# A decoder layer on one core: the last attention half by token tiles, and the sorted experts' fetches paced

## The chip, the cores and the metric

The kernel runs on one core of a Trainium2 chip. The metric is the device time of one execution in microseconds (us), the median of the runs shown; smaller is better.

## What is computed

The reference is one decoder layer for 2 x 512 tokens of width 512, all in float32:

```python
x = layernorm(x + ssm(x))                       # linear recurrence over the tokens
x = layernorm(x + cross_attention(x, context))  # 16 heads, 8 key heads, 1024 keys
h = x + self_attention(rmsnorm(x, norm1_w))     # causal, rope, 16 heads, 4 key heads
x = layernorm(h + moe(rmsnorm(h, norm2_w)))     # and here:

logits = xt @ gate_w                            # 8 experts
topv, topi = top_k(logits, 2); probs = softmax(topv)
for e in range(8):
    y = (silu(xt @ w1[e]) * (xt @ w3[e])) @ w2[e]   # width 1024
    out += w[:, e:e+1] * y                      # w: probs where e was chosen, else 0
```

## The kernel before

Matrix products are made of fp16 pairs: every operand is split into a high and a low fp16 part, and three products (high-high, high-low, low-high, `PAIRS`) are added in PSUM. So each operand costs a copy by ScalarE (high part), a subtraction by VectorE or GpSimd (low part), and, where it has to be turned, a DMA transpose issued by SyncE (SP). Every engine's program is written out by hand in Bass, with semaphores; nothing is scheduled by a tool. Phases (ssm, cross attention, self attention, routing, experts) end at a barrier.

**Self attention** (`attention`, called as "sa") works by halves: a half `h` is one key head `kv` and one sequence `b`, with four query heads (`groups`) of four token tiles of 128 (`TPB`), so `NS` = 16 steps `j`. A step makes the scores of one head and tile (`scores`, L1145, width 128 to 512 by the causal mask), the mask with the row's minimum (VectorE L1485), the exponential (ScalarE L1298), the reciprocal (L1446), its scale on GpSimd (L1007), the high part of the probabilities `PN` (ScalarE L1276) and the low one (VectorE L1453), and SP turns them into `PT` (L931). After every fourth step `values` (L1157) multiplies one head's turned probabilities with V, six steps (`TAIL`) behind; ScalarE (L1313) and VectorE (L1502) split the result into `OT`. A half also does jobs for its neighbours in fixed slots: the next half's projections, and the output of the half before (`output`, L1112), one tile of four heads a job, added to X by VectorE (`output_add`, L1435). In the last half (h = 7) there are no projections; the output of half 6 stands at `late_slots`, with three heads ahead (`parts_at`, steps 5 to 7) and the fourth later. WO of key head 3 is split in steps 0 to 3 of it (ScalarE L1281, GpSimd L981).

The half's own output can be finished only when all four heads are done, since `values` goes head by head: `first_parts` and `last_output` (L1121) gather it in four banks. Then for each tile: addition (L1435), mean square (ScalarE L1347, `row_square`), scale (GpSimd L1072 and L1074, `row_scale`), scaled row (VectorE L1524, `row_norm`), high part (ScalarE L1352, `row_high`), low part (VectorE L1530, `row_low`), turning by SP (L971), logits on TensorE (L1223) and the top two on VectorE (L1536 to L1543, `best_two`). Tiles 0 to 3 are sequence 0, whose rows are complete earlier; 4 to 7 are sequence 1. Before the turning, SP issues `next_loads`, the first expert's W1 and W3 (4 MB, L967, into `first`).

**Routing** ranks the choices. **The experts** (`phase_moe_routed`) are sorted by the number of their tokens, into places p = 0 to 7 with capacities of 352 down to 240 rows; the text calls them experts 1 to 8. GpSimd scatters the rows to DRAM (16 indirect DMAs, L1891) and then adds eight tiles (L1894). For each expert SP loads W13 of the next one (L1860), its rows (L1839), W2 (L1866), turns the rows (L1850) and stores the results (L1877). A step of an expert is `f`, one eighth of the width 1024: TensorE (L1936), Silu (ScalarE L2009), W2's high part (L2011), the product (VectorE L2067), W2's low part (L2070), and both parts of the result (L2019, L2078). The down projection (L1954, L1950) follows, tile by tile. In the last expert the results aren't stored but brought back by a matrix of `chosen` rows (VectorE L2084, turned by SP at L1872, L1972), while the other experts' rows are gathered from DRAM (16 indirect DMAs, L1907) and added by `combine` (L2055, L2058: tile t needs `gathered[t]`). `finish_rows` (L2117 to L2122) adds the last part and takes the statistics of the layer norm.

## Time and profile before

| | us |
|---|---|
| median of 3 runs | 1466.82 (1466.47 to 1468.64) |
| the profiled execution | 1465.96 |
| its span | 1464.3 |
| PE busy in it | 1324.5 (90%) |
| DVE, ACT, POOL busy | 1027.5, 808.1, 373.4 |
| mean granted clock of TensorE | 0.96 of full |

PE is the matmul engine TensorE, DVE is VectorE, ACT ScalarE, POOL GpSimd, SPq SP's queue of DMA issues. A row of a timeline gives the start in us from the beginning of the span, the time of the instruction or of several merged ones (x12), line and tiles (out<-in, buffer numbers left out), and in brackets how long the engine had been idle and what ended that. Matmuls overlap in the rows: twelve in a row are shown some 0.16 us longer than the distance to the next start. A label of a release is inferred from semaphores and can name the wrong DMA.

### The profile page before, as it was taken

The page shows a single profiled execution, that of the slowest core. Times are in us where ns is not written, and L with a number is a line of the kernel's source. Part 1 is how long each engine was busy: PE and PEld are TensorE (multiplying, and loading weights), DVE is VectorE, ACT ScalarE, POOL GpSimd, SP SyncE. Part 2 cuts the span into 40 slices and gives each one's busy share as a digit, 9 for nine tenths or more (in the row PEclk, how much of TensorE's full clock was granted, in tenths as well). Part 3 has the DMA queues.
Part 4 walks back from the last instruction along what each step waited for, and adds up shares of the span by engine and source line. Part 5 has one row for each costly group of instructions (what it writes and reads, how often), then busy time and mean ns, then how long its engine had stood idle before and what let it go on. Part 6 is the DMA issues. An engine that isn't in the chain of part 4 may idle for free. (4 is left out here: it accounts for less than half of the span.)

```text
span 1464.3 us, 24568 instructions
## 1 busy us (share of the span) xinstructions
PE 1324.5 (90%) x7943; PEld 715.8 (49%) x7943; DVE 1027.5 (70%) x1958; ACT 808.1 (55%) x1460; POOL 373.4 (25%) x610
## 2 busy tenths in 40 slices
PE   7988999999999999998688999998857999999965
PEld 4443444444444444443344555454434556666652
DVE  5847777777777777777568787878667556566646
ACT  5547666666666666665356565757523444555422
POOL 5402020202020202013456473645227000000042
PEclk9999999999999999999789999999878999999978
DMA  8327767676666666694643535335476646566751
GB/s 246 58 63 132 151 112 143 116 147 115 142 122 137 122 132 127 129 180 95 235 85 70 136 64 131 72 74 106 92 213 242 204 144 207 200 222 226 228 153 59
DMA packets 451836, 206.18 MB, mean 141 GB/s; under 512 B 401056, under 2 KB 415392, under 8 KB 451744
## 3 DMA queue, kind: packets, MB, share of 16 engines
q1 hardware_dynamic: 448608, 196.67, 56.9%
q0 software_dynamic: 2560, 8.39, 1.9%
q8 instruction: 44, 0.72, 0.2%
q14 instruction: 48, 0.39, 0.1%
q10 hardware_dynamic: 576, 0.00, 0.0%
HBM read 87.38 MB, written 16.45 MB: 71 GB/s over the span
## 5 line engine op out<-in xcount | busy, mean ns | idle before, releaser
L1453 DVE SCALAR_TENSOR_TENSOR X<-xa_SC,xa_rs,X 128x1024 f16<-128x1024 f32 x128 | 164.3, 1283 | 98.3 <-issue 97.6
L1276 ACT ACTIVATE X<-xa_SC,xa_rs 128x1024 f16<-128x1024 f32 x128 | 147.1, 1149 | 110.5 <-POOL xa_rs L1007 110.5
L1145 PE MATMUL xa_psS<-xa_KT,xa_QT 128*128 128x512 f16 x768 | 186.4, 379 | 6.0 <-DVE xa_mn L1485 4.6
L1157 PE MATMUL xa_psO<-wide,xa_V 128*128 128x512 f16 x768 | 173.8, 383 | 7.2 <-DMA wide<-X 6.9
L1007 POOL TENSOR_SCALAR xa_rs<-xa_rc,flag 128x1 f32<-128x1 f32 x128 | 33.9, 265 | 517.0 <-DVE xa_rc L1446 517.0
L1485 DVE CUSTOM_DVE_ANT_0 xa_SC<-xa_psS,maskb 128x1024 f32<-128x1024 f32 x128 | 155.0, 1211 | 4.5 <-PE xa_psS L1145 2.4
L1298 ACT ACTIVATE xa_SC<-xa_SC,xa_mn 128x1024 f32<-128x1024 f32 x128 | 145.4, 1136 | 13.4 <-DVE xa_mn L1485 13.3
L1936 PE MATMUL rmoe_psG<-rmoe_XGT,W 128*128 128x352 f16 (+6 forms) x768 | 112.9, 298 | 17.1 <-DVE zeros L2067 8.1
L1157 PEld LDWEIGHTS xa_psO<-wide,xa_V 128*128 128x128 f16 x768 | 74.5, 98 | 102.6 <-issue 17.5
L1936 PE MATMUL rmoe_psU<-rmoe_XGT,W 128*128 128x352 f16 (+6 forms) x768 | 112.7, 296 | 7.1 <-issue 7.0
L1145 PEld LDWEIGHTS xa_psS<-xa_KT,xa_QT 128*128 128x128 f16 x768 | 73.3, 98 | 90.7 <-DVE xa_mn L1485 9.4
L1298 ACT ACTIVATE sa_SC<-sa_SC,sa_mn 128x128 f32<-128x128 f32 (+3 forms) x128 | 71.4, 558 | 79.2 <-DVE sa_mn L1485 79.1
L1954 PE MATMUL rmoe_psY<-W,rmoe_HT 128*128 128x512 f16 (+3 forms) x456 | 99.9, 379 | 0.8 <-DVE rmoe_HT L2078 0.8
L1088 PE MATMUL xa_psJ<-XT,xa_WP 128*128 128x512 f16 x384 | 89.9, 385 | 11.0 <-POOL xa_WP L981 8.4
L1936 PEld LDWEIGHTS rmoe_psG<-rmoe_XGT,W 128*128 128x128 f16 x768 | 76.0, 100 | 46.0 <-DVE zeros L2067 9.4
L1088 PE MATMUL sa_psJ<-XT,first 128*128 128x512 f16 x384 | 92.4, 394 | 5.8 <-PEq L57 3.9
L1112 PE MATMUL sa_psJ<-sa_WO,sa_OT 128*128 128x512 f16 x336 | 79.5, 386 | 15.2 <-POOL sa_WO L981 7.0
L1453 DVE SCALAR_TENSOR_TENSOR sa_PN<-sa_SC,sa_rs,sa_PN 128x128 f16<-128x128 f32 (+3 forms) x128 | 77.5, 606 | 21.8 <-issue 9.9
L1936 PEld LDWEIGHTS rmoe_psU<-rmoe_XGT,W 128*128 128x128 f16 x768 | 76.3, 99 | 32.9 <-issue 8.8
L1112 PE MATMUL xa_psJ<-xa_WO,xa_OT 128*128 128x512 f16 x360 | 87.6, 379 | 0.0
L1485 DVE CUSTOM_DVE_ANT_0 sa_SC<-sa_psS,causal 128x128 f32<-128x128 f32 (+3 forms) x128 | 61.8, 483 | 36.1 <-PE sa_psS L1145 32.4
L1276 ACT ACTIVATE sa_PN<-sa_SC,sa_rs 128x128 f16<-128x128 f32 (+3 forms) x128 | 71.0, 555 | 27.2 <-POOL sa_rs L1007 24.8
(291 smaller groups left out, 2273.9 us busy)
## 6 DMA issues: line engine op xcount, KB each, us to landing
first<-in_L_ffn_w_dram SPq DMA_DIRECT2D x14, 2048.0 KB, 11.9
W2raw<-in_L_ffn_w_dram SPq DMA_DIRECT2D x8, 2048.0 KB, 9.1
expert_rows_dram<-zeros SPq DMA_DIRECT2D x10, 512.0 KB, 9.7
xa_WPraw<-in_L_xattn_Wq_dram SPq DMA_DIRECT2D x8, 512.0 KB, 11.1
xa_WOraw<-in_L_xattn_Wo_dram SPq DMA_DIRECT2D x8, 512.0 KB, 4.7
first<-in_L_ffn_wq_dram SPq DMA_DIRECT2D x4, 1024.0 KB, 8.0
first<-in_L_ffn_wo_dram SPq DMA_DIRECT2D x4, 1024.0 KB, 5.7
first<-in_L_ffn_w_dram SPq DMA_DIRECT2D x8, 512.0 KB, 6.8
```

What stands on the lines that cost most here:

```text
L1007: nc.gpsimd.tensor_scalar(rs[:, j % 4:j % 4 + 1], rc[:, j % 4:j % 4 + 1], unit, 1.0, ALU.mult, ALU.mult).then_inc(scale_done, 1)
L1088: last = nc.tensor.matmul(bank[:, :], wq_v[:, hw, k, a, :], XT[:, hx, k, b * S:(b + 1) * S], start=(q + k == 0), stop=(q == 2 and k == DC ...
L1112: last = nc.tensor.matmul(bank[:, :], OT[b][:, ho, g, t * P:(t + 1) * P], WO[:, hw, g, :], start=(g + q == 0), stop=(g == groups - 1 and q ...
L1145: last = nc.tensor.matmul(psS[j % NSC][:, c:c + cw], QT[b][:, hq, g, t * P:(t + 1) * P], KT[b][:, hk, c:c + cw], start=(q == 0), stop=(q = ...
L1157: last = nc.tensor.matmul(psO[:, c:], V[b][:, hv, blk, :], PT[g % NPT][:, blk, hp, c:], start=(blk + q == 0), stop=(blk == NBLK - 1 and q ...
L1276: nc.scalar.activation(PN[j % NPN][:, 0:w // P, 0, :], by_block(SC[j % NSC], w), ACT.Identity, scale=rs[:, j % 4:j % 4 + 1]).then_inc(norm ...
L1298: nc.scalar.activation(SC[j % NSC][:, 0:w], SC[j % NSC][:, 0:w], ACT.Exp, bias=mn[:, j % 4:j % 4 + 1], scale=-1.0, accum_out=sm[:, j % 4:j ...
L1453: nc.vector.scalar_tensor_tensor(out=PN[j % NPN][:, 0:w // P, 1, :], in0=by_block(SC[j % NSC], w), scalar=rs[:, j % 4:j % 4 + 1], in1=PN[j ...
L1485: nc.vector.tensor_tensor_reduce(out=SC[j % NSC][:, 0:w], in0=psS[j % NSC][:, 0:w], in1=mask_of(b, j % TPB), scale=-SCORE_SCALE, scalar=3e ...
L1936: last = nc.tensor.matmul(bank[f % 2][:, 0:c], W13[:, hw, w, k, f * P:(f + 1) * P], XGT[:, hx, k, 0:c], start=(i + k == 0), stop=(i == 2 a ...
L1954: last = nc.tensor.matmul(psY[y][0:w, :], HT[:, hh, k, r * P:r * P + w], W2[:, hw, k, :], start=(i + k == 0), stop=(i == 2 and k == FC - 1))
```

## The change

It has two parts. In the self attention's last half the steps go by token tile: `step_of` gives tile 3 with its four heads first, then tiles 2, 1 and 0. `tile_values` multiplies one tile of all four heads, `own_output` makes its output one tile later, and square, scale, norm, parts and logits of the tiles follow in tables of steps (`square_at` and so on); the order of the tiles in them is `tile_of`. The turned probabilities of tiles 3 and 1 lie in `first`, so `next_loads` wait for the third tile's values. The output of half 6 is made whole, in slots 8 to 11.

In the experts, the second expert's W13 is fetched in four pieces, each after the one before; the rows of the next expert are turned ahead of W2's fetch; `chosen` is made and turned in experts 2 to 5 in place of the last; a tile's gathers wait for those two tiles before; and `combine` is spread over the last expert and behind it. ScalarE waits for W2 after the first Silu.

```diff
@@ attention
-    late_slots = {8: ([("wo", 0)], []), 9: ([("wo", 1)], []), 10: ([("wo", 2)], []), 12: ([("wo", 3)], [])}
-    parts_at = {5: 0, 6: 1, 7: 2}
+    late_slots = {8 + t: ([("wo", t)], []) for t in range(TPB)}
...
+        PT_last = PT if route is None else [
+            ap.bitcast(F16).rearrange("p (k l c) -> p k l c", l=2, c=S)
+            for ap in (route[-1][:, 0:NBLK * S], turned[:, 0].rearrange("p t d -> p (t d)"))]
...
-            square_at = (11, 12, 13, 14)
+            tile_of = [0, 1, 2, 3, 7, 6, 5, 4]
...
+            own_bank = [psJ[i] for i in (1, 0, 2, 1)]
+            square_at = {10: 0, 11: 1, 12: 2, 13: 3, 16: 4, 18: 5, 20: 6}
+            high_at = {14: 0, 15: 1, 16: 2, 17: 3, 18: 4, 19: 5}
+            scale_at = {11: 0, 12: 1, 13: 2, 14: 3}
+            own_at = {15: 0, 17: 1, 20: 2}
+            norm_at = {13: 0, 14: 1, 15: 2, 16: 3, 17: 4, 18: 5}
+            low_at = {14: 0, 15: 1, 16: 2, 17: 3, 18: 4, 20: 5}
...
+        def step_of(m, last):
+
+            j = m % NS
+            return (j % groups, TPB - 1 - j // groups) if by_tile(m, last) else (j // TPB, j % TPB)
...
@@ SyncE, attention
                 sp.wait_ge(wo_done, kv_heads * NWO)
-                sp.wait_ge(job_ready, jobs_before(last_h))
+                sp.wait_ge(pv_ready, last_h * groups + 3)
                 for dst, src, arrived in next_loads:
                     sp.dma_start(dst, src).then_inc(arrived, 16)
-                for i in range(NT):
-                    sp.wait_ge(xp_lo, i + 1)
+                for n, i in enumerate(tile_of):
+                    sp.wait_ge(xp_lo, n + 1)
...
@@ TensorE, attention
+            def tile_values(h, b, u):
+
+                for q in range(TPB):
+                    pe.wait_ge(landed[q], 16 * (h * groups + u + 1))
+                wait_from(pe, o_lo, h * groups + u)
+                t = TPB - 1 - u
+                for blk in range(t + 1):
+                    for q, (hv, hp) in enumerate(PAIRS):
+                        last = nc.tensor.matmul(psO[:, :], V[b][:, hv, blk, :], PT_last[u % NPT][:, blk, hp, :],
+                                                start=(blk + q == 0), stop=(blk == t and q == 2))
+                last.then_inc(pv_ready, 1)
+
+            def own_output(h, b, u):
+                output(h, b, TPB - 1 - u, last_job(TPB + u), own_bank[u], NJ, h * groups + u)
...
-                    if causal and last and j in parts_at:
-                        k = parts_at[j]
-                        pe.wait_ge(wo_done, kv_heads * NWO)
-                        output(h - 1, 1 - b, k, jobs_before(h) + k, psJ[BANK[b][k]], jobs_back(h, k, last),
-                               range(groups - 1))
                     m = j - TAIL
                     if m % TPB == TPB - 1 and (m >= 0 or not first):
-                        values(head_of(h, m), b if m >= 0 else 1 - b, (m % NS) // TPB)
+                        if by_tile(m, last):
+                            if m // TPB == TPB - 1:
+                                logits(0)
+                            tile_values(h, b, m // TPB)
+                        else:
+                            values(head_of(h, m), b if m >= 0 else 1 - b, (m % NS) // TPB)
+                        if by_tile(m, last) and m > TPB:
+                            own_output(h, b, m // TPB - 1)
...
@@ SyncE, experts
                     for i, w in enumerate((w1, w3)):
-                        sp.dma_start(W13raw[:, i, :, :], w[bass.ds(named[p], 1)].rearrange("o (k p) f -> p (o k) f", p=P)).then_inc(w13_in, 16)
+                        rows = w[bass.ds(named[p], 1)].rearrange("o (k p) f -> p (o k) f", p=P)
+                        if first:
+                            for k in range(0, DC, 2):
+                                wait_from(sp, w13_in, 16 * (2 * i + k // 2))
+                                sp.dma_start(W13raw[:, i, k:k + 2, :], rows[:, k:k + 2, :]).then_inc(w13_in, 16)
+                        else:
+                            sp.dma_start(W13raw[:, i, :, :], rows).then_inc(w13_in, 16)
...
                     load_rows(p + 1)
+                    turn_rows(p + 1)
                     sp.wait_ge(w2_done, FC * (p + 1))
                     sp.dma_start(W2raw[:], w2[bass.ds(named[p], 1)].rearrange("o (k p) d -> p (o k) d", p=P)).then_inc(w2_in, 16)
-                    turn_rows(p + 1)
-                if last:
-                    for t in range(NT):
+                if p in choose_at:
+                    for t in choose_at[p]:
                         sp.wait_ge(chosen_done, t + 1)
...
@@ GpSimd, experts
             for t in range(NT):
+                if t >= 2:
+                    pool.wait_ge(gathered[t - 2], 32)
                 for k, dst in enumerate((Y1, Y2)):
                     pool.indirect_dma_start(out=dst[:, t, :], out_offset=None, in_=YG[0:ROWS, :],
...
@@ VectorE, experts
+                    if p in choose_at and f < len(choose_at[p]):
...
                     if last and f >= FC // 2:
-                        for t in range(2 * f - FC, 2 * f - FC + 2):
-                            combine(t)
+                        combine(f // 2 - 2, f % 2)
+                if last:
+                    combine(2)
+                    combine(3)
                 for r in range(TILES[p]):
                     if last:
...
-                        if r:
+                        if r == 0:
+                            for t in range(4, 7):
+                                combine(t)
+                        else:
                             finish_rows(r - 1)
...
             over_experts(dve, step)
+            combine(NT - 1)
             for t in range(TILES[LAST] - 1, NT):
                 finish_rows(t)
```

`choose_at` is two tiles in each of the places 1 to 4.

The order of TensorE's program at the end of the last half, before (`sa_psO` are values, `sa_WO` outputs, `sa_GWP` logits; four rows of values are one head):

```order
L1157 MATMUL sa_psO<-wide,sa_V 128x128 x3
L1121 MATMUL sa_psS<-sa_WO,sa_OT 128x512 x3
L1121 MATMUL sa_psJ<-sa_WO,sa_OT 128x512 x3
L1121 MATMUL sa_psS<-sa_WO,sa_OT 128x512 x3
L1121 MATMUL sa_psJ<-sa_WO,sa_OT 128x512 x15
L1223 MATMUL sa_psS<-sa_GWP,XT 128x8 x84
L1223 MATMUL sa_psO<-sa_GWP,XT 128x8 x12
```

and the same place now:

```order
L1206 MATMUL sa_psS<-sa_KT,sa_QT 128x128 x6
L1177 MATMUL sa_psO<-first,sa_V 128x512 x6
L1143 MATMUL sa_psJ<-sa_WO,sa_OT 128x512 x12
L1196 MATMUL sa_psS<-sa_GWP,XT 128x8 x48
L1177 MATMUL sa_psO<-wide,sa_V 128x512 x3
L1143 MATMUL sa_psJ<-sa_WO,sa_OT 128x512 x24
L1196 MATMUL sa_psS<-sa_GWP,XT 128x8 x36
L1196 MATMUL sa_psO<-sa_GWP,XT 128x8 x12
```

All logits stood behind all values and outputs; now those of the first four tiles (x48) stand ahead of the last tile's values (x3) and of the last two outputs (x24).

SP's program in the loop's place 2 (it fetches for the next expert, of 304 rows), before:

```order
L1860 DMA first<-in_L_ffn_w_dram 128x4x1024 x2
L1839 DMA X<-expert_rows_dram 128x2x512
L1842 DMA X<-expert_rows_dram 48x512
L1866 DMA W2raw<-in_L_ffn_w_dram 128x8x512
L1850 DMA_TRANSPOSE rmoe_XGT<-X 128x8x128 x3
L1877 DMA expert_out_dram<-X 128x512 x2
```

and now:

```order
L1925 DMA first<-in_L_ffn_w_dram 128x4x1024 x2
L1898 DMA X<-expert_rows_dram 128x2x512
L1901 DMA X<-expert_rows_dram 48x512
L1909 DMA_TRANSPOSE rmoe_XGT<-X 128x8x128 x3
L1932 DMA W2raw<-in_L_ffn_w_dram 128x8x512
L1937 DMA_TRANSPOSE wide<-wide 128x3x128 x2
L1942 DMA expert_out_dram<-X 128x512 x2
```

The turning of the rows stands ahead of W2's fetch, and two transposes of `chosen` (`wide`) have come in behind it.

## Rows read from the trace of the kernel before

**Rows 1.** The page, its first line.

```profile
span 1464.3 us, 24568 instructions
```

**Rows 2.** Windows: us, busy us by engine, granted clock, DMA share, GB/s.

```profile
1068.00:1090.00 22.00, 4.97 (x133) 4.25 (x133) 12.25 (x55) 3.77 (x10) 4.63 (x29) 0.61 0.86 192
...
1392.00:1429.00 37.00, 25.59 (x193) 20.27 (x194) 16.57 (x35) 8.25 (x20) 15.70 (x16) 0.77 0.56 143
```

**Rows 3.** Timeline of PE in the last half: start, us, what, idle before.

```profile
1026.16 4.02 PE L1112 MATMUL sa_psJ<-sa_WO,sa_OT 128*128 128x512 f16 x9 [7.02 <-POOL sa_WO L981]
...
1042.86 2.75 PE L1112 MATMUL sa_psJ<-sa_WO,sa_OT 128*128 128x512 f16 x12
```

**Rows 4.** Timeline of SP's queue behind the last half.

```profile
1057.48 4.11 SPq L967 DMA_DIRECT2D first<-in_L_ffn_w_dram  x8
1061.70 17.87 SPq L971 DMA_TRANSPOSE XT<-wide  x8
```

**Rows 5.** Timeline of DVE: norm and low parts of the first four tiles.

```profile
1056.57 1.40 DVE L1524 SCALAR_TENSOR_TENSOR wide<-X,sa_rr,sa_wb 128x512 f32<-128x512 f32 x2
...
1059.08 2.49 DVE L1530 TENSOR_TENSOR wide<-wide 128x512 f16<-128x512 f32 x4
```

**Rows 6.** Timeline of PE: logits of the first and the fourth tile.

```profile
1071.78 0.44 PE L1223 MATMUL sa_psS<-sa_GWP,XT 128*128 128x8 f16 x12 [4.22 <-DMA XT<-wide]
...
1076.87 0.48 PE L1223 MATMUL sa_psS<-sa_GWP,XT 128*128 128x8 f16 x12 [2.45 <-DMA XT<-wide]
```

**Rows 7.** Timeline of DVE: last addition, last low part, top two.

```profile
1069.46 0.68 DVE L1435 TENSOR_TENSOR X<-sa_psJ,X 128x512 f32<-128x512 f32 x1
...
1074.31 0.69 DVE L1530 TENSOR_TENSOR wide<-wide 128x512 f16<-128x512 f32 x1 [0.68 <-ACT wide L1352]
...
1082.68 0.16 DVE L1543 FIND_INDEX8 idx<-top,lg 128x8 uint32<-128x8 f32 x1
```

**Rows 8.** Timelines of ACT, DVE, POOL and PE in the first expert.

```profile
1118.29 0.46 ACT L2009 ACTIVATE ropeC<-rmoe_psG 128x352 f32<-128x352 f32 x1 [5.23 <-DMA wide<-sa_PN]
...
1119.29 10.63 DVE L2070 TENSOR_TENSOR W<-W2raw,W 128x512 f16<-128x512 f32 x1
...
1119.56 9.80 POOL L1894 TENSOR_TENSOR X<-X 128x512 f32<-128x512 f32 x8
...
1130.85 3.55 PE L1936 MATMUL rmoe_psG<-rmoe_XGT,W 128*128 128x352 f16 x12 [7.51 <-DVE zeros L2067]
```

**Rows 9.** Timelines of PE and SP's queue at the start of expert 8.

```profile
1392.02 1.41 PE L1936 MATMUL rmoe_psG<-rmoe_XGT,W 128*128 128x240 f16 x12 [2.37 <-DMA rmoe_XGT<-X]
...
1381.49 8.48 SPq L1850 DMA_TRANSPOSE rmoe_XGT<-X  x2
```

**Rows 10.** Timelines of ACT, PE, SP's queue and POOL in expert 8.

```profile
1403.63 0.37 ACT L2009 ACTIVATE ropeC<-rmoe_psG 128x240 f32<-128x240 f32 x1 [5.25 <-DMA wide<-sa_PN]
...
1418.05 0.37 ACT L2009 ACTIVATE ropeS<-rmoe_psG 128x240 f32<-128x240 f32 x1 [13.19 <-DMA wide<-sa_PN]
...
1410.19 0.76 PE L1936 MATMUL rmoe_psU<-rmoe_XGT,W 128*128 128x240 f16 x3 [1.95 <-issue]
...
1434.41 5.99 PE L1954 MATMUL rmoe_psY<-W,rmoe_HT 128*128 128x512 f16 x27 [0.83 <-DVE rmoe_HT L2078]
...
1397.11 25.76 SPq L1872 DMA_TRANSPOSE wide<-wide  x8
...
1414.17 0.95 POOL L1907 DMA_INDIRECT XT<-expert_out_dram,rmoe_slots  x1 [0.30 <-issue]
```

**Rows 11.** Groups by line and form, 1389 to 1441: busy us, mean ns.

```profile
L2055 DVE SCALAR_TENSOR_TENSOR X<-wide,p,X 128x512 f32<-128x512 f32 x8 | 6.0, 745 | 0.0
```

**Rows 12.** Windows, columns as rows 2: during the sixteen scatters.

```profile
1104.00:1108.00 4.00, 4.00 (x19) 2.20 (x18) 3.82 (x7) 1.42 (x3) 3.69 (x2) 0.65 0.34 131
```

**Rows 13.** DMA issues: what, count, KB each, median us to landing.

```profile
expert_out_dram<-X SPq DMA_DIRECT2D x14, 256.0 KB, 2.5
...
XT<-wide SPq DMA_TRANSPOSE x8, 3.3
```

More of the change, by code:

```diff
@@ L1104, in project, with output @@
                 last.then_inc(job_ready, 1)
-            def output(h, b, t, job, bank, back=NJ, gs=range(groups)):
-                pe.wait_ge(o_lo, h * groups + gs[-1] + 1)
+            def output(h, b, t, job, bank, back=NJ, head=None):
+                pe.wait_ge(o_lo, (h + 1) * groups if head is None else head + 1)
                 wait_from(pe, job_free, job - back + 1)
-                for g in gs:
+                for g in range(groups):
                     for q, (ho, hw) in enumerate(PAIRS):
@@ L1137, in first_parts, with logits @@
                     last_output(t, early)
+            def tile_values(h, b, u):
[10 more added lines that the diff above has]
+                output(h, b, TPB - 1 - u, last_job(TPB + u), own_bank[u], NJ, h * groups + u)
+            def logits(n):
+                lo, hi, bank = choice[n]
+                if n == 0:
+                    pe.wait_ge(gw_done, 1)
+                    pe.wait_ge(masked, (last_h + 1) * NS)
+                first_tile = min(tile_of[lo:hi])
+                for i in tile_of[lo:hi]:
+                    pe.wait_ge(xt_in[i], 16)
+                    for q, (hx, hw) in enumerate(PAIRS):
+                        for k in range(DC):
+                            at = (i - first_tile) * E
+                            last = nc.tensor.matmul(bank[:, at:at + E], XT[:, hx, k, i * P:(i + 1) * P], GWP[:, hw, k, :],
+                                                    start=(q + k == 0), stop=(q == 2 and k == DC - 1))
+                last.then_inc(logits_ready, 1)
             def scores(n, b, g, t, j):
@@ L1168, in jobs @@
                         pe.wait_ge(wo_done, (kv + b) * NWO)
-                        output(h - 1, 1 - b, i, job, psJ[BANK[b][k]], jobs_back(h, k, last),
-                               range(groups - 1, groups) if causal and last and i in parts_at.values() else range(groups))
+                        output(h - 1, 1 - b, i, job, psJ[BANK[b][k]], jobs_back(h, k, last))
             def half(h, kv, b, first, last):
@@ L1479, in half @@
                     if j < NS:
-                        w = width(j % TPB)
+                        t = step_of(j, last)[1]
+                        w = width(t)
                         dve.wait_ge(scores_ready, n + 1)
@@ new lines, in half, with own_add, row_norm @@
+                    if last and route is not None and j in own_at:
+                        own_add(own_at[j])
+                    if last and route is not None and j in norm_at:
+                        row_norm(norm_at[j])
+            def own_add(u):
+                output_add(last_h, 1, TPB - 1 - u, last_job(TPB + u), own_bank[u])
+            def row_norm(n):
+                if n == 0:
+                    dve.wait_ge(wb_in, 16)
+                if n == 7:
+                    dve.wait_ge(xp_lo, 5)
+                dve.wait_ge(rr_done, n + 1)
+                dve.wait_ge(job_free, last_job(n) + 1)
+                nc.vector.scalar_tensor_tensor(out=xw[n], in0=X[:, tile_of[n], :], scalar=rr[:, n:n + 1], in1=wb[:],
@@ L1541, in best_two @@
                 dve.wait_ge(top_done, n + 1)
-                for i in range(lo, hi):
+                for i in tiles:
                     last = nc.vector.max_index(idx[:, i, :], top[:, i, :], lg[:, i, :])
@@ L2385, in decoder_layer @@
                   turned=wide[:, :, TPB:, :],
-                  route=(norm2_w, XW, XP, gate_w, lg, top, idx, next_loads, zeroed, 16 * len(cleared), kept))
+                  route=(norm2_w, XW, XP, gate_w, lg, top, idx, next_loads, zeroed, 16 * len(cleared), kept, first))
         W13 = sb("W13", [P, 2, 2, DC, F], F16)
```

250 lines of the change are left out of this document (120 added, 130 removed).

## The prediction

> **What bounds the kernel now.** I read the page first: one core, span 1464.3 us [rows 1]. The profiled execution took 1465.96 us, 1.7 over its span and 0.9 under the median of 1466.82; the sum is made against 1465.96, and 0.9 is added at the end. A measurement of this kernel tells a change from none from about 0.2%, 2.9 us.
>
> The chain of waits runs through TensorE for most of the experts, and the table by stage says where it does not: in 1068 to 1090 PE works 4.97 of 22 us, and in 1392 to 1429, the last expert, 25.59 of 37 [rows 2]. I therefore read the timelines around these two and at the two ends of the change. The reader is to see five things. (a) In the last half of the self attention PE stands 7.02 us for the split of WO (POOL L981), and its next nine matmuls take 4.02 us; twelve take 2.75 elsewhere, 2.59 or 0.216 each from start to start [rows 3]. (b) SP issues the 4 MB of the first expert's weights from 1057.48 and the turned rows of the norm behind them; though four tiles were ready at 1061.6 (DVE L1530 ends), they reach PE only at 1071.78 (first) and 1076.87 (fourth) [rows 4, 5, 6]. (c) From the last output's addition to the end of the top two there are 13 us in which almost nothing but latency passes [rows 7]. (d) In the first expert ScalarE gets its third step 5.23 us late, and one DVE instruction of some 0.69 us takes 10.63, as long as POOL's eight additions beside it [rows 8]. (e) Expert 8 starts 2.37 us late for its rows [rows 9], then ScalarE stands 5.25 and 13.19 us on something the trace can't name (the transposes in the label were long over), with PE doing single matmuls between "issue" gaps; SP's eight transposes of `chosen` and POOL's sixteen gathers are in flight then [rows 10].
>
> **The sum, part by part.** A, B, C, D are the terms.
>
> *A, attention by tiles.* Softmax, values and outputs hold the same columns as before; only their order moves. The stall of 7.02 us goes, since no output stands at step 5 any more. What is late next: the four widest tiles now come first, each with a piece of WO, at some 1.9 us a step (ScalarE 0.72 + 0.61 + 0.51), then four at 1.3; DVE has the last head of the half before at about 1029.3. Only then can PE's first output begin. From there PE is full: four outputs at 2.59, values 2.59 and 1.94, the first own output 2.59, scores 1.5, and 1.7 for the half clock after the idle time (row 1026.16: 9 matmuls 4.02 for 1.94, less what a shorter idle time saves): 20.7, so 1050.0. DVE then has four masks, reciprocals and low parts of width 128 (2 us), the low part of OT 0.6, four low parts and three norms of rows at 0.62 and 0.70 [rows 5], one addition: 6.8, so 1056.8. SP turns the last tile (1.2) and begins the loads at 1058.1, where it was 1057.48: the time won at (a) is used up, **+0.6**.
>
> The price is behind that. `next_loads` now wait for the third tile's values because that tile lies in their destination, and `logits(0)` stands ahead of `tile_values` of the last tile in PE's program. It needs the turned rows of four tiles, which stand behind 4 MB in SP's order. Before, the fourth was there 1076.87 - 1057.48 = 19.4 us after the first load [rows 4, 6]; nothing about the loads has changed, so I take 19.4. Before, PE had no attention work left behind this wait. Now all of the following stands there: logits 0.5; values and own output 2, 15 matmuls at 0.216 plus 2.0 for the half clock, 5.3 (25.2 so far); addition 0.7, square 0.8 (ScalarE has it ahead of OT's high part), OT high 0.6, low 0.65 (27.9); own output 3, 2.6; addition 0.7 (31.2); square to low part 4.9, the interval from 1070.14 to 1075.00 [rows 7]; turning 3.5, as XT's 3.3 [rows 13] and a semaphore; logits 0.5 and top two 0.7: 41.0 after the first load. Before: 1082.84 - 1057.48 = 25.4. **A = 0.6 + 15.6 = +16.2 us.** Bounds: if XT's rows weren't held, PE would take PV at 1061 and the chain end at 79.9, A = -2.9; if the first load begins 6 us later than reckoned (steps at 2.2), +22.
>
> *B, first expert.* The 4 MB for expert 2 come in four pieces, one at a time. If ScalarE's third step is no longer late, DVE has multiplied step 3 (0.53) before POOL's additions begin at 1119.56, and PE does step 5 in their shadow; the next begins where step 5 began, 1130.85 [rows 8]. That is one step of two groups of 1.8 (expert 8's 1.23 by 352/240 columns), **-3.6**. Bounds 0 and -7.5 (PE's whole idle time). The additions themselves stay. For these the Trainium skill (SBUF — State Buffer, "SBUF: two separate sides") says that DVE and GpSimd take the shared port for one whole instruction and the other blocks; by that a DVE instruction would wait one addition of 1.2 us, and B would be near -7.5. The row shows it blocked through all eight, and the measurement decides.
>
> *C, rows turned ahead of W2.* Expert 8's 2.37 us go: its transposes took 8.48 us in issue behind 2 MB of W2 [rows 9]. **-2.4**; W2 itself is issued some 3 us later (2 or 3 transposes at 1.3) and has the down projection, 10.4 us or more, to land in before ScalarE's first piece, which now comes after the first Silu: nothing. The two transposes of `chosen` in experts 2 to 5 stand before the stores of YR and the next W13 load, but the turning ahead of them no longer stands behind W2 either: I put SP 1 us later there, ahead of loads that have a whole up projection to land, at nothing (at most 1 us at each of four experts). DVE's `chosen`, 0.42 each, lies in PE's steps of 3.1 to 3.6.
>
> *D, last expert.* From 1392.02 PE needs eight steps of 2.46 (two groups of twelve matmuls, 1.41 less an overlap of 0.18 [rows 9]) and 48 matmuls of 0.216, 19.7 + 10.4 = 30.1; it ended at 1440.24 (1434.41 + 5.99 less the overlap [rows 10]), 48.2 later: 18.1 too much. Two causes: the waits of (e), and DVE's four `combine` in each of the steps 4 to 7 (3.0 us beside 1.3 of other work, against 2.46 of PE). Both go: one combine (0.75) beside the 1.3 fits into 2.46; tiles 2 to 6 fall under the down projection; tile 7's two, 1.4, come on DVE's last chain [rows 11]. **-18.1 + 1.4 = -16.7.** The transposes are gone from here, and scatters of the same form alone kept the DMA engines 0.34 busy, while PE ran full [rows 12]; so I take the waits as gone. Bounds: +1.4 (all stay) and -16.7. The pacing allows two tiles in flight. A gather's landing isn't shown; stores of the same 256 KB took 2.5, turned rows 3.3 [rows 13]. Up to 3.3 the window of two tiles costs nothing (POOL issues one tile in 2.5); at 5 it gives a tile each 3.75, tile 6 at 1425 in place of 1418, and costs 6.
>
> Sum: 16.2 - 3.6 - 2.4 - 16.7 = **-6.5**: 1459.5, with 0.9 a median of **1460**.
>
> **Rivals.** (1) *The rows aren't held:* XT lands soon after its issue, as PN does. Against it [rows 4, 6]. It gives -2.9 - 22.7 = -25.6, 1441.
> (2) *Slower: instructions still come late in the last expert.* If the gathers from POOL alone, and not they with the transposes, keep ScalarE and PE waiting, the 18.1 us stay: +16.2 - 6.0 + 1.4 = +11.6, 1479. It decides once more than 9.4 of the 18.1 stay. For it: ScalarE's long wait (1404.9 to 1418.05) ends 3 us after the last gather was issued. Against it: [rows 12].
> (3) *The window is too narrow:* gathers take 5 us, +6, 1466.
> (4) *Pacing does nothing for another queue:* each DMA engine takes turns between queues, so ScalarE's wait in expert 1 would not depend on how many pieces of W13 stand behind each other; B is 0: 1464. The Trainium skill states such turns (DMA: Bandwidth & Descriptors, "Queues, rings and completion order": "each SDMA engine round-robins between the queue rows it has work for, at *packet* granularity"). No row of the trace before tells the two apart.
>
> **How the numbers follow.** My forecast 0.45, its own range 1451 to 1469 (A by 5 either way, B by 4); rival 1 0.15, rival 2 0.15, rival 3 0.10, rival 4 0.10; 0.05 for a first load far later. Faster by over 2.9: four fifths of mine, rival 1, half of 4, a little of 3: 0.58. Slower by over 2.9: rival 2, a tenth of mine, some of 3 and the 0.05: 0.24. Within: 0.18. The range leaves out half of rival 1 and most of 2: 1441 to 1474.
>
> **What would show it.** First W13 load at 1055 to 1061; PE idle some 17 us before `logits(0)`, with the last tile's values behind it; top two end near 1099. After that everything counted from there: expert 2's up projection 3.6 us sooner, no PE idle time ahead of expert 8, no "issue" rows in it, PE 30 us from its first up to its last down matmul, and finish_rows(7) some 45 us after its start. If the rows of four tiles are there before the third tile's values end, A is wrong; if ScalarE stands in expert 8, D is.

## The result and the profile after

The changed kernel took 1480.54 us (median of 4 runs, 1478.91 to 1482.74) against 1466.64 for the kernel before, measured beside it: a ratio of 1.0103 (95% interval 1.0079 to 1.0127). It is slower by 1%, where I forecast 1460 and put 0.24 on slower. The profiled execution took 1478.91.

The page after, its first line; before it was 1464.3 [rows 1], so 12.7 us are to be found:

```profile
span 1477.0 us, 24551 instructions
```

The two traces have the same landmarks, and the 12.7 us are the differences of the stretches between them:

| stretch | before | after | change | forecast |
|---|---|---|---|---|
| A: to the end of the top two | 1082.84 | 1104.63 | +21.8 | +16.2 |
| B: from there to expert 1's end | 75.88 | 72.24 | -3.6 | -3.6 |
| C: from there to expert 8's first matmul | 233.30 | 230.40 | -2.9 | -2.4 |
| D: expert 8, first up to last down matmul | 48.22 | 43.75 | -4.5 | -18.1 |
| D: from there to the end | 24.06 | 25.98 | +1.9 | +1.4 |

A single stretch has some play: in the other traces of this record the top two end at 1099.6 to 1103.8 with the changed attention (e1, e14, e16) and at 1082.7 to 1086.7 with that of before (e2, e5 to e8, e10 to e12). So A is some 13 to 22 us, and 21.8 between these two traces; e1's time (19.4 us over before, with 3.2 won back in B) speaks for the upper end.

**A.** PE's timeline after, at the end of the attention (start, us, what, idle before):

```profile
1033.29 2.75 PE L1143 MATMUL sa_psJ<-sa_WO,sa_OT 128*128 128x512 f16 x12 [2.06 <-issue]
...
1055.29 2.75 PE L1143 MATMUL sa_psJ<-sa_WO,sa_OT 128*128 128x512 f16 x12
1079.46 0.46 PE L1196 MATMUL sa_psS<-sa_GWP,XT 128*128 128x8 f16 x12 [21.42 <-DMA XT<-wide]
...
1082.98 0.48 PE L1196 MATMUL sa_psS<-sa_GWP,XT 128*128 128x8 f16 x12 [0.85 <-DMA XT<-wide]
1083.33 1.44 PE L1177 MATMUL sa_psO<-wide,sa_V 128*128 128x512 f16 x3
1084.56 4.23 PE L1143 MATMUL sa_psJ<-sa_WO,sa_OT 128*128 128x512 f16 x12
1091.54 4.14 PE L1143 MATMUL sa_psJ<-sa_WO,sa_OT 128*128 128x512 f16 x12 [2.75 <-DVE sa_OT L1553]
...
1103.47 0.49 PE L1196 MATMUL sa_psO<-sa_GWP,XT 128*128 128x8 f16 x12 [5.92 <-DMA XT<-wide]
```

and SP's queue beside it:

```profile
1053.36 10.97 SPq L957 DMA_TRANSPOSE wide<-sa_PN  x4
1064.43 4.03 SPq L993 DMA_DIRECT2D first<-in_L_ffn_w_dram  x8
1068.58 33.02 SPq L997 DMA_TRANSPOSE XT<-wide  x8
```

PE stands 21.4 us ahead of `logits(0)`, with the last tile's values, two outputs and half of the rows' chain behind it in its program. The fourth tile's rows came 18.55 us after the first load (19.4 before, [rows 4, 6]).

**B.** DVE's timeline after, in the first expert:

```profile
1141.43 10.26 DVE L2137 TENSOR_TENSOR W<-W2raw,W 128x512 f16<-128x512 f32 x1
```

and PE's:

```profile
1152.62 3.51 PE L2003 MATMUL rmoe_psG<-rmoe_XGT,W 128*128 128x352 f16 x12 [5.07 <-DVE causal L2134]
```

DVE is blocked through POOL's eight additions as in [rows 8]; PE's idle time is 5.07 in place of 7.51, and it has one step more behind it when it comes.

**D.** PE's timeline after, in expert 8:

```profile
1407.27 1.39 PE L2003 MATMUL rmoe_psG<-rmoe_XGT,W 128*128 128x240 f16 x12
...
1421.24 0.47 PE L2003 MATMUL rmoe_psU<-rmoe_XGT,W 128*128 128x240 f16 x3 [0.18 <-issue]
1422.64 0.47 PE L2003 MATMUL rmoe_psU<-rmoe_XGT,W 128*128 128x240 f16 x3 [0.93 <-issue]
...
1424.07 0.57 PE L2003 MATMUL rmoe_psU<-rmoe_XGT,W 128*128 128x240 f16 x4 [0.44 <-issue]
1429.91 2.28 PE L2003 MATMUL rmoe_psG<-rmoe_XGT,W 128*128 128x240 f16 x10 [5.27 <-DVE causal L2134]
1433.22 0.36 PE L2003 MATMUL rmoe_psG<-rmoe_XGT,W 128*128 128x240 f16 x1 [1.03 <-issue]
...
1440.66 10.52 PE L2021 MATMUL rmoe_psY<-W,rmoe_HT 128*128 128x512 f16 x48
1451.02 1.03 PE L2039 MATMUL rmoe_psG<-X,wide 128*128 128x512 f16 x4
```

ACT's, the Silu of the steps 5 and 6:

```profile
1429.04 0.37 ACT L2071 ACTIVATE ropeC<-rmoe_psG 128x240 f32<-128x240 f32 x1 [9.38 <-DMA wide<-sa_PN]
...
1435.52 0.37 ACT L2071 ACTIVATE ropeS<-rmoe_psG 128x240 f32<-128x240 f32 x1 [5.24 <-DMA wide<-sa_PN]
```

POOL's, the first and the last of the sixteen gathers:

```profile
1412.75 1.00 POOL L1974 DMA_INDIRECT wide<-expert_out_dram,rmoe_slots  x1 [259.44 <-DMA expert_out_dram<-X]
...
1432.09 0.95 POOL L1974 DMA_INDIRECT XT<-expert_out_dram,rmoe_slots  x1 [0.30 <-issue]
```

Expert 8 starts without idle time, and the transposes of `chosen` are gone from it. Yet the same picture as in [rows 10] is back: single matmuls between "issue" gaps and ScalarE late without a cause that the trace names (at 1429.04 PE's product had been complete since 1424.6), from 8 us after the first gather's issue to 3 us after the last one's.

### The profile page after: what moved, and what is told of

The parts are those of the page before. It is cut to its first block and busy times, and to the rows that moved or that the text cites. A ratio compares the mean times of both kernels' runs of the same rounds, so it can differ in the third digit from the quotient of the medians.

```text
span 1477.0 us, 24551 instructions
## 1 busy us (share of the span) xinstructions
PE 1324.3 (90%) x7925; PEld 716.1 (48%) x7925; DVE 1027.6 (70%) x1958; ACT 808.2 (55%) x1460; POOL 371.7 (25%) x610
## 5 line engine op out<-in xcount | busy, mean ns | idle before, releaser
L1351 ACT ACTIVATE xa_SC<-xa_SC,xa_mn 128x1024 f32<-128x1024 f32 x128 | 145.4, 1136 | 14.4 <-DVE xa_mn L1535 14.3
L1143 PE MATMUL sa_psJ<-sa_WO,sa_OT 128*128 128x512 f16 x384 | 91.0, 388 | 13.3 <-DVE sa_OT L1553 8.7
L1502 DVE SCALAR_TENSOR_TENSOR sa_PN<-sa_SC,sa_rs,sa_PN 128x128 f16<-128x128 f32 (+3 forms) x128 | 77.1, 602 | 20.9 <-issue 10.6
L2003 PEld LDWEIGHTS rmoe_psU<-rmoe_XGT,W 128*128 128x128 f16 x768 | 75.5, 98 | 26.8 <-issue 3.6
L1329 ACT ACTIVATE sa_PN<-sa_SC,sa_rs 128x128 f16<-128x128 f32 (+3 forms) x128 | 71.1, 555 | 28.5 <-POOL sa_rs L1033 26.4
```

The source lines that it names most:

```text
L1143: last = nc.tensor.matmul(bank[:, :], OT[b][:, ho, g, t * P:(t + 1) * P], WO[:, hw, g, :], start=(g + q == 0), stop=(g == groups - 1 and q ...
L1329: nc.scalar.activation(PN[j % NPN][:, 0:w // P, 0, :], by_block(SC[j % NSC], w), ACT.Identity, scale=rs[:, j % 4:j % 4 + 1]).then_inc(norm ...
L1351: nc.scalar.activation(SC[j % NSC][:, 0:w], SC[j % NSC][:, 0:w], ACT.Exp, bias=mn[:, j % 4:j % 4 + 1], scale=-1.0, accum_out=sm[:, j % 4:j ...
L1502: nc.vector.scalar_tensor_tensor(out=PN[j % NPN][:, 0:w // P, 1, :], in0=by_block(SC[j % NSC], w), scalar=rs[:, j % 4:j % 4 + 1], in1=PN[j ...
L2003: last = nc.tensor.matmul(bank[f % 2][:, 0:c], W13[:, hw, w, k, f * P:(f + 1) * P], XGT[:, hx, k, 0:c], start=(i + k == 0), stop=(i == 2 a ...
```

## Experiments

Theories at the start: **held rows** (A is the time for which the 4 MB hold the rows, times PE's order), **gathers** (my rival 2: the gathers alone keep PE and ScalarE waiting), against **steps** (A is lost in the half itself) and **transposes and gathers together** (my forecast). The runs were made in five groups, each with its own runs of the kernel before; ratios are to these. Stage D means expert 8 from its first up to its last down matmul.

### The two parts apart

e1 keeps the changed attention and takes the experts from before; e2 the reverse. The edit is one half of the change's diff each: e1 leaves out all hunks on the experts, e2 all on the attention.

> The changed attention with the experts of before. Theory H (held rows): the whole loss is made in the attention; the top two end 21.7 us later than before (1082.84 to 1104.56 in the two traces) and nothing of it comes back, so 1466.6 + 21.7 = 1488. Rival: part of the 21.7 us overlaps with waits of the old experts (the first expert's idle 7.5 us), then 1480 to 1484.

> The attention of before with the changed experts. If the two parts add: the traces give 12.7 - 21.7 = -9.0, so 1466.6 - 9.0 = 1457.6, with 3.6 of it in the first expert, 2.9 ahead of expert 8 and 2.5 in and behind it. Rival: the gain in the first expert came only from the shifted place of the scatters in time; then 1461.

e1: 1485.3, ratio 1.0135 (1.01 to 1.0171); e2: 1459.8, 0.9954 (0.994 to 0.9968); the kernel before in this group 1465.89. The loss is the attention's and the experts' part does win. In e1 the top two end at 1103.78, 20.9 later than before, and stretch B is 72.7, that is 3.2 shorter than before **with the old experts**. PE's timeline in e1's first expert:

```profile
1142.77 1.96 PE L1994 MATMUL rmoe_psG<-rmoe_XGT,W 128*128 128x352 f16 x12 [0.72 <-DVE zeros L2125]
...
1151.53 3.70 PE L1994 MATMUL rmoe_psG<-rmoe_XGT,W 128*128 128x352 f16 x12 [5.01 <-DVE causal L2125]
```

and SP's, where both halves of the next W13 go out at once:

```profile
1133.62 0.54 SPq L1918 DMA_DIRECT2D first<-in_L_ffn_w_dram  x2
```

ScalarE waited long once here too (4.25 us), one step later, where it costs PE 0.72. In e2, with the pacing, it waited 5.18 us and PE 0.67. Nor is the pacing enough: e7 and e12 (below) have it, their third step comes late as before (waits of 5.73 and 5.72 us), and B is 75.7 and 75.5 as before. So B's 3.6 us aren't shown to come from the pacing: which of ScalarE's steps is late decides, and that differs from kernel to kernel. With the third late B is 75.5 to 75.9 (before, e7, e12), with the fourth 72.7 to 73.2 (e1, e2, e3). C's 3 us do come with the experts' part: 233.4 in e1, 230.4 in every kernel that has it. Stage D is 48.4 in e1 and 44.1 in e2.

### What held the attention

e3 issues the loads behind four tiles' turning; e4 moves the logits behind the outputs.

```diff
@@ e3: SyncE
-                for dst, src, arrived in next_loads:
-                    sp.dma_start(dst, src).then_inc(arrived, 16)
                 for n, i in enumerate(tile_of):
+                    if n == 4:
+                        for dst, src, arrived in next_loads:
+                            sp.dma_start(dst, src).then_inc(arrived, 16)
                     sp.wait_ge(xp_lo, n + 1)
@@ e4: TensorE
                         if by_tile(m, last):
-                            if m // TPB == TPB - 1:
-                                logits(0)
                             tile_values(h, b, m // TPB)
...
-                for n in range(1, len(choice)):
+                for n in range(len(choice)):
                     logits(n)
```

In e4 VectorE's `best_two(0)` and `best_two(1)` move behind `row_low(7)` as well.

> The changed kernel with the 4 MB of the first expert issued behind the turning of the first four tiles' rows. Theory H: the rows land some 1.3 us apart from 1065 on, logits(0) run at about 1070 in place of 1079 to 1083, and the last tile's values follow; the rows of the next tiles are then held to about 19 us behind the first load (1070 + 19 = 1089). Top two end near 1092, 12 us sooner: 1468. Rival S (the rows are late for another reason than the loads, for example the transposes' own queue): PE idles to 1079 as now, 1480.

> The changed kernel with logits(0) behind the last own output in TensorE's program, and the top two of all tiles at the end of VectorE's. Theory H: the loads still hold the rows, but values and outputs of the last tiles run beside them, so the end is 25.4 us behind the first load as before: 1064.4 + 25.4 = 1089.8, 14.7 us sooner than 1104.56: 1466. Rival S: the last rows stay late for their own chain (addition, square, scale, low part), and the top two end at about 1100: 1476.

e3: 1468.79, ratio 1.0014 (0.9997 to 1.0032); e4: 1463.46, 0.9986 (0.997 to 1.0001). The top two end at 1093.4 and 1090.5 in place of 1104.6. PE's timeline in e3, the logits of the first and the fourth tile:

```profile
1066.88 0.46 PE L1197 MATMUL sa_psS<-sa_GWP,XT 128*128 128x8 f16 x12 [9.87 <-DMA XT<-wide]
...
1070.94 0.48 PE L1197 MATMUL sa_psS<-sa_GWP,XT 128*128 128x8 f16 x12 [0.81 <-DMA XT<-wide]
```

and in e4, the last tile's values and the first logits:

```profile
1066.90 1.44 PE L1177 MATMUL sa_psO<-wide,sa_V 128*128 128x512 f16 x3 [8.13 <-DVE sa_OT L1551]
...
1079.79 0.44 PE L1196 MATMUL sa_psS<-sa_GWP,XT 128*128 128x8 f16 x12 [0.39 <-DMA XT<-wide]
```

With the loads behind them, the first rows reach PE 3.4 us after their transpose's issue (SP at 1063.47) in place of 10.9: it is the 4 MB that hold them. With the logits last the hold costs PE nothing, and the end is 25.4 us after the first load (1090.54 - 1065.13), the interval of the kernel before. Held rows and TensorE's order are shown for 14.1 of A's 21.8 us (1104.63 less 1090.54); the other 7.7 are the late first load, and these are lost in the half itself, as "steps" had it. e15 is e4 with the row work two steps later:

```diff
-            square_at = {10: 0, 11: 1, 12: 2, 13: 3, 16: 4, 18: 5, 20: 6}
-            high_at = {14: 0, 15: 1, 16: 2, 17: 3, 18: 4, 19: 5}
+            square_at = {10: 0, 11: 1, 12: 2, 13: 3, 16: 4, 18: 5, 21: 6}
+            high_at = {16: 0, 17: 1, 18: 2, 19: 3, 20: 4, 21: 5}
...
-            norm_at = {13: 0, 14: 1, 15: 2, 16: 3, 17: 4, 18: 5}
-            low_at = {14: 0, 15: 1, 16: 2, 17: 3, 18: 4, 20: 5}
+            norm_at = {15: 0, 16: 1, 17: 2, 18: 3, 19: 4, 20: 5}
+            low_at = {16: 0, 17: 1, 18: 2, 19: 3, 20: 4, 21: 5}
```

> The kernel of e4_logits_last with norm, high and low part of the rows of tiles 0 to 3 two steps later each (1 step for the square of the third own tile). Theory V (VectorE's and ScalarE's work on these rows, in between the masks and low parts of the last tile, makes the first load 7 us later than before): the last tile's turning ends some 3 us sooner, first load at about 1062 in place of 1065.1, and since the rows held behind it end 25.4 us after it, 1460. Rival: the first load is late for TensorE's outputs ahead of it; then it stays at 1065 and the time at 1463.

e15 ran in the fourth group: 1444.35, ratio 0.997 (0.9956 to 0.9983). SP's queue in e14 of the same group (with the rows' work where the change has it):

```profile
1050.53 10.96 SPq L957 DMA_TRANSPOSE wide<-sa_PN  x4
1061.59 4.00 SPq L993 DMA_DIRECT2D first<-in_L_ffn_w_dram  x8
```

and in e15:

```profile
1050.19 7.44 SPq L957 DMA_TRANSPOSE wide<-sa_PN  x4
1057.74 4.33 SPq L993 DMA_DIRECT2D first<-in_L_ffn_w_dram  x8
```

The turning of the last tile waited for its own low parts, which stood behind norms and low parts of rows on VectorE; without them it takes 3.5 us less. The first load comes 3.9 sooner, and 3.5 of that is the edit's: from the end of the first own output to the first load it is 12.3 us in the change, e4, e14 and e16, and 8.8 in e15 and e18. The top two end 25.5 us behind it again.

### What keeps the last expert waiting

All of these start from e2. e5 leaves the gathers out, e6 and e7 change the window, e8 and e12 fetch the same bytes plainly, e10 and e11 keep fewer gathers in flight. e5, e8 and e12 leave out or replace the rows that the layer needs, so they tell where time goes and are no kernels to keep; each has two runs:

```diff
@@ e6 (e7: neither line)
-                if t >= 2:
-                    pool.wait_ge(gathered[t - 2], 32)
+                if t >= 1:
+                    pool.wait_ge(gathered[t - 1], 32)
@@ e11
+                lag = 1 if t < 5 else 2
+                if t >= lag:
+                    pool.wait_ge(gathered[t - lag], 32)
@@ e10, with a semaphore for each k and t
                 for k, dst in enumerate((Y1, Y2)):
+                    if t >= 1:
+                        pool.wait_ge(gathered[k][t - 1], 16)
@@ e12 in place of the indirect DMA; e8 the same by SyncE
+                    at = (2 * t + k) * P
+                    pool.dma_start(dst[:, t, :], YG[at:at + P, :]).then_inc(gathered[t], 16)
```

> The kernel of e2_experts_only without its sixteen gathers (what is left out: the rows of the other experts aren't fetched, the additions take what lies in their buffers). Theory G: the gathers alone keep TensorE and ScalarE waiting in the last expert; from its first up matmul to the end of the down projection 30 us in place of 44.1, no issue rows, 1459.8 - 14 = 1446. Rival: the instructions come late for another reason (the place in the program); the stage stays at 44 and the time at 1459.

> The kernel of e2_experts_only with the gathers of one tile in flight in place of two. Theory Q (what waits behind the gathers waits the longer the more of them are outstanding): the stage shrinks from 44.1 to about 38, 1454. Rival T (only the bytes moved count): the stage stays within 1 us of 44.1; and if a tile's round trip gets longer than its 2.5 us of issue, the gathers end later and the time goes up to 1463.

> The kernel of e2_experts_only with all gathers issued without a wait, as before the change. Theory Q: the stage grows from 44.1 to 47 or more (it was 48.2 before, with the transposes beside the gathers), 1463. Rival T: 44.1 and 1460; then the 4.1 us came from the transposes and the spread additions alone.

> The kernel of e2_experts_only with sixteen plain fetches of 256 KB from SyncE's queue in place of the gathers, two tiles in flight (the rows fetched are not the chosen ones). If the bytes on the DMA engines are what keeps the others waiting (T): the stage stays near 44. If it is the kind of transfer that GpSimd issues row by row: the stage is near 30 and the time near 1446, as without gathers.

> The kernel of e2_experts_only with each gather waiting for the one two before it, so that two gathers are in flight all the time (in e6_one_tile two were issued and both had to land). Theory W (how many gathers stand in the queue decides): TensorE runs as in e6_one_tile, 30 us from its first up to its last down matmul, and the gathers need 16 x 2.0 = 32 us in place of 42, so the end comes 8 us sooner than in e6: 1450. Rival: a steady stream of gathers does what four in flight do, issue rows come back and the time stays at 1457 to 1460.

> The kernel of e2_experts_only with one tile in flight for the first five tiles and two for the last three, which fall into and behind the down projection. Theory W: TensorE is not held in the up projection, the last gather lands some 7 us sooner than in e6_one_tile: 1451. Rival: the last three tiles hold the down projection's instructions and the time stays at 1457.

> The fetches of e8_plain_fetches issued by GpSimd in place of SyncE (the rows fetched are not the chosen ones). If a transfer whose packets GpSimd's own queue moves is what delays the others: issue rows in the last expert and about 1459. If only the indirect form does: 30 us for the stage and 1446, as in e8.

| kernel | gathers in flight | stage D | from D to the end | median | ratio (interval) |
|---|---|---|---|---|---|
| e5 | none | 30.04 | 25.6 | 1444.77 | 0.9841 (0.9817 to 0.9865) |
| e6 | 2, both to land | 30.04 | 40.7 | 1457.63 | 0.9926 (0.9908 to 0.9943) |
| e7 | no limit set | 44.87 | 26.4 | 1462.04 | 0.9962 (0.9949 to 0.9976) |
| e8 | plain, SyncE | 30.04 | 26.1 | 1445.59 | 0.9847 (0.9823 to 0.9871) |
| e10 | 2, rolling | 30.04 | 30.1 | 1447.56 | 0.9869 (0.9837 to 0.99) |
| e11 | 2, from tile 5 on 4 | 30.04 | 33.5 | 1451.99 | 0.9893 (0.9876 to 0.9909) |
| e12 | plain, GpSimd | 30.04 | 26.2 | 1446.38 | 0.9852 (0.9832 to 0.9872) |

Without gathers the stage takes the 30.04 us that TensorE needs. So the 14 us of e2 are theirs alone, as rival 2 had it. (Before the change the stage took 48.2 us, and 48.4 in e1; the 3.5 more than e7's 44.87, which also sets no limit, belong to the transposes of `chosen` or to the four additions a step, which no run tells apart.) It is not their bytes: e8 moves the same 4.2 MB at the same place, and e12 even through the same queue and with the same number of packets. The DMA view of e12, 1392 to 1425 (packets, MB, share of 16 engines; KB each, us to landing):

```profile
q0 software_dynamic: 1280, 4.20, 40.6%
...
wide<-expert_out_dram POOLq DMA_DIRECT2D x8, 256.0 KB, 3.3
```

and of e2, 1394 to 1418:

```profile
q0 software_dynamic: 1280, 4.20, 61.4%
...
wide<-expert_out_dram,rmoe_slots POOLq DMA_INDIRECT x8
```

The indirect form, issued as fast as in e2 and e7, delays PE and ScalarE; with two in flight it doesn't. I had expected a slope (38 us in e6, 47 or more in e7), and that was wrong. e2's window and no window differ by only 0.8 us (44.06, 44.87), but they are nearly the same experiment: the sixteen issues of e2 span 19.6 us and those of e7 19.1, so a window of four hardly held anything back. In e6 and e10 the number in flight and the pace fall together (one gather in 2.6 and 1.9 us in place of 1.3), and no run tells which of the two matters. For plain fetches the pace doesn't: e8 and e12 issue theirs in 14.4 and 16.4 us. What is won is partly paid at the end (column four; e6's profiled execution took 1462.76, 5 over its median), since fewer in flight take longer, and the last tiles' additions stand ahead of `finish_rows`. PE's timeline behind stage D in e6:

```profile
1435.05 1.03 PE L1981 MATMUL rmoe_psG<-X,wide 112*128 112x512 f16 x2 [13.64 <-DVE X L2103]
```

and in e10:

```profile
1421.89 1.04 PE L1981 MATMUL rmoe_psG<-X,wide 112*128 112x512 f16 x2 [4.67 <-DVE X L2103]
```

In e6 a tile takes 5.1 to 5.5 us (1400.92, 1406.04, 1411.25, 1416.75), in e10 a gather lands 3.7 us after its issue and one goes out every 1.9.

### Half the loads, and both

e9 is e2 with W1 (4 of the 8 loads) ahead of the turning of the rows and W3 behind it; e13 and e17 are e9 with e10's gathers.

```diff
-                for dst, src, arrived in next_loads:
+                for dst, src, arrived in next_loads[:DC]:
                     sp.dma_start(dst, src).then_inc(arrived, 16)
                 for i in range(NT):
...
+                for dst, src, arrived in next_loads[DC:]:
+                    sp.dma_start(dst, src).then_inc(arrived, 16)
```

> The kernel of e2_experts_only (attention of before) with W1 of the first expert (2 MB) issued where all 4 MB were, and W3 behind the last turning of rows. Theory H: half the bytes hold the rows half as long; the first four tiles' rows land near 1069, the last ones some 4 us behind their low part, and the top two end 3 to 4 us sooner; W3 lands before the experts begin: 1459.8 - 3.5 = 1456. Rival: W3 lands too late for ScalarE's split and the gain is given back, 1459 to 1461.

e9: 1457.19, ratio 0.9928 (0.9911 to 0.9944); the top two end at 1081.45, 21.7 after the first load, where it was 25.4 before and 27.2 in e2. Stretch B is 71.8 as in e10 (71.9), so W3 isn't late. The intervals of e9 and e2 (another group) overlap at their ends, so the times alone don't show the gain; the traces do: from the first load to the top two it is 21.6 to 21.9 us in e9, e13 and e17, and 24.7 or more in all nine with the whole 4 MB ahead and the attention of before.

> e9_half_the_loads and e10_rolling_two together: the attention of before with half of the first expert's loads behind the rows, the changed experts with two gathers always in flight. The two edits lie 300 us apart, so they should add: 1447.6 - 2.6 = 1445. Rival: the last expert begins at another point of the instruction stream and some of the wait comes back, 1448 or more.

> The changed kernel with two gathers always in flight, nothing else. If what the gathers cost doesn't depend on the attention: as e2_experts_only to e10_rolling_two, 12.2 us less: 1480.5 - 12.2 = 1468, still level with before, the 21.7 us of the attention being left. Rival: less than 8 us, because the cost depends on where the expert's stage falls: 1472 to 1476.

e13: 1443.98, ratio 0.9964 (0.9952 to 0.9976); e14: 1464.69, ratio 1.0116 (1.0093 to 1.0139). Both are measured against a kernel before that took **1449.36 us** in this group (23 runs, 1445.21 to 1453.52), not 1467. None of its three traces (e13, e14, e15) shows late instructions in the last expert, e15 with the changed kernel's own window of two tiles included (of the kernel before there is no trace in it):

```profile
1405.48 10.52 PE L2017 MATMUL rmoe_psY<-W,rmoe_HT 128*128 128x512 f16 x48
```

(its first up matmul was at 1385.80, so stage D is 30.04). I took this for a property of the chip and ran three kernels on another:

> The kernel of e14_after_rolling once more. The chip of e14 ran the kernel before in 1449 us in place of 1467 and its last expert without a wait, with four gathers in flight too, so nothing could be won there. If this chip has the wait (before near 1467): 1468, 12 us under the changed kernel's 1480.5, ratio to before 1.001. If it is such a chip again (before near 1449): ratio 1.012 as in e14.

> The kernel of e13_both once more. On a chip with the wait: 1445, ratio to before 0.985. On one without it: ratio 0.996 as in e13, all of it from the experts' first and eighth and the halved loads.

> The kernel of e15_rows_later (attention by tiles, logits last, rows of the first four tiles two steps later) with two gathers always in flight: the changed kernel with its three costs taken out. On a chip with the wait: e4's 1463.5 less 3.5 for the rows and less 12.2 for the gathers, 1448, ratio 0.987. On one without it: no better than e15, ratio 0.997 to 0.998.

The kernel before again took 1449.74 (19 runs), on the chip on which it had taken 1465.89 in the first group. e16: 1466.25, ratio 1.0123 (1.0106 to 1.014); e17: 1444.74, 0.9971 (0.9961 to 0.9981); e18: 1448.36, 0.9989 (0.9972 to 1.0005). So it is no property of a chip. Whatever it is, the wait is there for all runs of a group or for none, as far as traces and times show.

It isn't confined to the gathers either. In the first expert the sixteen scatters are in flight, and ScalarE's longest wait ahead of POOL's additions is 2.9 us or more in ten of the fourteen traces that have the wait (before, e1 to e3, e5, e7, e9 to e12). In all six traces of the last two groups (e13 to e18) it is 2.04. The Silu of the third step in e7 and in e15:

```profile
1118.87 0.46 ACT L2011 ACTIVATE ropeC<-rmoe_psG 128x352 f32<-128x352 f32 x1 [5.73 <-PE rmoe_psU L1943]
1115.90 0.46 ACT L2067 ACTIVATE ropeC<-rmoe_psG 128x352 f32<-128x352 f32 x1 [2.04 <-PE rmoe_psU L1999]
```

So the 5.23 us of [rows 8] are most likely the same delay, caused by scatters; no run leaves the scatters out, so that isn't shown.

Where the wait is absent, the rolling gathers cost time: from stage D to the end it is 29.1 to 30.4 us in e13, e14, e16, e17 and e18 and 26.1 in e15, and PE waits 3.5 to 4.8 us for the last additions in the five, 1.0 in e15. Keeping two in flight is an insurance. Whether it cures the wait in the changed kernel itself wasn't measured, since neither group of e14 and e16 had the wait.

Without the wait e13 (0.9964), e17 (0.9971) and e15 (0.997) beat both kernels; with it the best measured that computes the layer is e10 (0.9869).

## Why the prediction was wrong

**Forecast 1460, measured 1480.5: 20 us, of which 5.6 lie in A and 14.1 in D.** The other terms stand in size.

*D failed at one step*: "The transposes are gone from here, and scatters of the same form alone kept the DMA engines 0.34 busy, while PE ran full [rows 12]; so I take the waits as gone." The 18.1 us too much were rightly counted (30.1 reckoned, 30.04 measured wherever nothing holds PE), and gone they would have given -18.1 as priced. But two things were in flight in [rows 10], transposes and gathers, and I took the pair as the cause, on the strength of a row about scatters. That row covers 4 us (1104 to 1108); at the end of the same scatters, at 1118.29, ScalarE was 5.23 us late [rows 8], so they were a sign for rival 2 and not against it. e5 shows the gathers alone to be the cause of the 14 us that e2 loses, and e8 and e12 that it isn't their bytes. Rival 2 had the mechanism, its deciding point (9.4 of 18.1 stay) was passed with 13.6, and it had 0.15; that its 1479 lies so near 1480.5 is partly luck, since it had all 18.1 stay, 4.5 too many, and A 5.6 too low; its evidence was in my own text: ScalarE's longest wait ended 3 us after the last gather.

*A: the larger half held, the smaller failed.* The rows of four tiles took 18.55 us from the first load (19.4 reckoned) and the top two 40.2 (41.0); e3 and e4 confirm the hold and the order, and so rival 1 is out. The first load was reckoned at 1058.1 and came at 1064.43. The sum had VectorE need 6.8 us from the first own output to the last low part; it took 11.0 (1052.08 to 1063.06). About 1 us of the gap is a slip in adding: the terms listed (2, 0.6, four at 0.62, three at 0.70, one addition) make 7.9. The rest is a wait put at nothing: 4.0 of the 11.0 us VectorE stands, 0.54, 1.14 and 1.75 of them for ScalarE's high parts, and ScalarE in turn for GpSimd's scale (2.51). e15 takes 3.5 us back. Another 2.1 came ahead of it: the first own output ended at 1052.08 in place of 1050.0. In e1, e3, e4, e14 and e16, with the same steps, it ended at 1049.3 to 1052.8, so these 2.1 lie within what executions differ by. My upper bound for this (+22 for "6 us later") is where A landed.

*B: right in size (-3.6), wrong in reason.* e1 has 3.2 of it without the pacing, and e7 and e12 have the pacing without the gain. Rival 4 (pacing does nothing) is thus the better account of B, though the time that it gave rested on B being 0. For the block of one DVE instruction the Trainium skill (SBUF — State Buffer, "SBUF: two separate sides") would have one addition of 1.2 us as its length; here it is 10.26 beside POOL's 9.82, as before, and the measurement decides again.

*C* came out at -2.9 for -2.4, the *tail* at +1.9 for +1.4. *Rival 3* (window too narrow) was wrong: at two tiles gathers went on every 1.25 to 1.4 us; at one tile it came true (e6).

## What to carry to other kernels

When a stall has two suspects in flight, its price isn't won by removing one of them: give each alone a chance of its own, and measure one alone first. A load placed ahead of small latency-bound transfers on a queue costs less (here some 3 us for 2 of the 4 MB, e9) as long as nothing else stands behind their consumer; a reorder that puts work behind that consumer turns the hidden wait into path, so look at what follows the waiting instruction in its own engine's program. And in an in-order engine that trades small pieces with others, reckon a chain with its handovers, not with the sum of its instructions.

## What was not expected of the hardware

- Sixteen indirect gathers of 256 KB, issued every 1.3 us with a window of four or none, delay the instructions of TensorE and ScalarE by some 14 us in all (stage D 44 us in place of 30.04); with two in flight, one every 1.9 us, or as plain fetches from either queue, they don't. The mechanism isn't settled. In the gaps PE starts single matmuls some 0.7 us apart (e1: 1431.71 and 1432.43), so its instructions seem to come in small portions. But what passes on the instruction queues in stage D is the same with the delay (e2) and without it (e15), three packets of 0.04 MB together, and the trace doesn't show what held anything back.
- That delay is absent in whole groups of runs: the kernel before took 1449.4 and 1449.7 us in two of them and 1465.9, 1467.6 and 1467.6 in three (and 1466.6 beside the change), one chip being in both kinds. The change itself wasn't run in such a group. An estimate of its loss there is 12 to 17 us: the differences of the two traces outside stage D make 21.8 - 3.6 - 2.9 + 1.9 = +17.2, and with rolling gathers it measured +15.3 and +16.5 (e14, e16), of which some 3.3 are their longer end.
